# Layer 1's class tokens become the stationary operand, the atoms' weights move in a new stream layout, and the degrees are summed behind the norm's statistics

## The reference

```python
patch_out = gelu(patch_tokens @ fc1_w.T + fc1_b) @ fc2_w.T + fc2_b
gate_logits = einsum('bnd,nrd->bnr', l2norm(cls_tokens), l2norm(gate_pair)) + balance_bias
route_probs = softmax(gate_logits);  chosen_route = argmax(route_probs)
hid_all = gelu(einsum('bnd,ahd->bnah', cls_tokens, atom_in_w) + atom_in_b)
route_candidates = einsum('bnrh,nrdh->bnrd', sh_pair, route_out_w) + atom_out_b[dst]
cls_out = chosen_cand * chosen_w
```

## Time and profile before

| | us |
|---|---|
| median of 3 runs | 3323.42 (3315.17 to 3325.01) |
| profiled execution | 3323.25 |
| its span, first to last instruction | 3321.4 |
| TensorE busy | 3084.2 |
| DVE busy | 1713.4 |
| GpSimd busy | 1428.0 |
| ScalarE busy | 757.8 |
| mean granted TensorE clock | 0.952 of full |

### The profile page before, as it was taken

The page is one execution under the profiler, slowest core; times in us unless marked ns, Lnnn a source line. Parts: engine busy times, 40 slices in busy tenths (PEclk is TensorE's granted clock), DMA queues, the critical chain, the costliest instruction groups (busy, mean ns, idle before and its releaser), DMA issues.

```text
span 3321.4 us, 39056 instructions
## 1 busy us (share of the span) xinstructions
PE 3084.2 (93%) x14137; PEld 2434.6 (73%) x14147; DVE 1713.4 (52%) x2812; ACT 757.8 (23%) x1342; POOL 1428.0 (43%) x1007
## 2 busy tenths in 40 slices
PE   8999899999999977998997889899999998989978
PEld 3567577888888865776786578578888886778858
DVE  7734699565555355547765436533334436641141
ACT  1043211233323221103153122111111112221222
POOL 2022287435443451563430034356666664536600
PEclk9999999999999988999988789999999999999987
DMA  2011266212221121221210231122332232213303
GB/s 81 15 48 43 91 200 218 67 48 77 72 62 58 62 81 59 75 93 54 66 48 10 71 110 60 56 86 90 99 96 94 94 95 67 67 48 100 99 31 132
DMA packets 92134, 259.38 MB, mean 78 GB/s; under 512 B 10431, under 2 KB 11071, under 8 KB 91716
## 3 DMA queue, kind: packets, MB, share of 16 engines
q1 hardware_dynamic: 80352, 219.45, 20.9%
q10 hardware_dynamic: 11652, 38.19, 3.3%
HBM read 256.03 MB, written 1.57 MB: 78 GB/s over the span
## 4 chain that ended last, share of the span: by engine, by line
PE 85%; DVE 9%; issue 3%; ACT 2%; DMA 0%; ACTq 0%; DVEq 0%
PE ps L429 22%; PE ps L433 21%; PE ps L434 21%; PE ps L911 2%; DVE aux L1982 2%; PE ps L537 1%; PE ps L531 1%; PE ps L1245 1%; PE ps L997 1%; PE ps L1141 1%; PE ps L801 1%; PE ps L783 1%; PE ps L790 1%; PE ps L775 1%; DVE hot L2423 1%
## 5 line engine op out<-in xcount | busy, mean ns | idle before, releaser
L367 POOL TENSOR_SCALAR w_hi<-raw 128x768 fp32r<-128x768 f32 x498 | 462.4, 929 | 1680.4 <-PE ps L429 1451.8
L370 POOL TENSOR_TENSOR w_lo<-raw,w_hi 128x768 fp32r<-128x768 f32 x498 | 974.3, 1956 | 41.5
L429 PE MATMUL ps<-H_hi,w_hi 128*128 128x512 f32 x804 | 318.9, 397 | 21.1 <-issue 11.6
L429 PE MATMUL ps<-A_hi,w_hi 128*128 128x512 f32 x780 | 309.0, 396 | 12.1 <-ACT scr L1570 12.1
L434 PE MATMUL ps<-H_hi,w_lo 128*128 128x512 f32 x804 | 315.9, 393 | 0.0
L433 PE MATMUL ps<-H_lo,w_hi 128*128 128x512 f32 x804 | 315.8, 393 | 0.0
L429 PE MATMUL ps<-B_hi,w_hi 128*128 128x512 f32 x720 | 291.7, 405 | 21.0 <-DVE B_lo L1776 14.9
L433 PE MATMUL ps<-A_lo,w_hi 128*128 128x512 f32 x780 | 305.7, 392 | 0.0
L434 PE MATMUL ps<-A_hi,w_lo 128*128 128x512 f32 x780 | 305.1, 391 | 0.0
L433 PE MATMUL ps<-B_lo,w_hi 128*128 128x512 f32 x720 | 282.9, 393 | 0.0
L434 PE MATMUL ps<-B_hi,w_lo 128*128 128x512 f32 x720 | 282.8, 393 | 0.0
(11 more groups left out here) (480 smaller groups left out, 5857.5 us busy)
## 6 DMA issues: line engine op xcount, KB each, us to landing
raw<-stream_dram SPq DMA_DIRECT2D x558, 384.0 KB, 3.0
w_ring<-w_dram ACTq DMA_DIRECT2D x45, 384.0 KB, 3.6
u_rows<-rows_dram ACTq DMA_DIRECT2D x8, 768.0 KB, 5.8
rows<-rows_dram ACTq DMA_DIRECT2D x7, 768.0 KB, 3.8
w_last<-w_dram ACTq DMA_DIRECT2D x9, 384.0 KB, 3.6
x<-x_dram ACTq DMA_DIRECT2D x1, 1536.0 KB, 9.0
out_dram<-x ACTq DMA_DIRECT2D x1, 1536.0 KB, 5.1
orf<-orf_dram ACTq DMA_DIRECT2D x6, 192.0 KB, 3.1
```

Of the source, the lines that this page charges most:

```text
L367: pool.tensor_scalar(w_hi[:, b // 3, b % 3], raw[:, b // 3, b % 3], 1.0, 1.0, ALU.mult, ALU.mult)\
L370: pool.tensor_tensor(w_lo[:, b // 3, b % 3], raw[:, b // 3, b % 3], w_hi[:, b // 3, b % 3], ALU.subtract)\
L429: mm = pe.matmul(o, wh, xh, start=first, stop=False, skip_group_check=True)
```

## The change

- **Up.** A block now holds, for one chunk of 128 features and one half h, 128 columns of fc1 and 480 columns of the atoms' first weights. The chunk's 8 token columns become the stationary operand, and the 480 weight columns move: the class tokens come out as rows, in [8, 480] of banks 2 and 3, summed over the six chunks. fc1 keeps its form (128x128 weights, 512 columns), but goes chunk by chunk, so it begins with the first normed chunk. The gates' matmuls stand behind the fourth block.
- **Between.** DVE copies the class rows out of PSUM, ten transposes bring them to [96, 80] in bank 5, DVE adds the biases there and ScalarE takes one GELU where it took ten. Four DVE operations apply the route weights where twelve did.
- **Down.** fc2 comes first, from two blocks. Then come ten blocks with 96 rows of use, 768 columns each: the 8 hidden columns are stationary, and the weights move in two halves of 384 columns into banks 0 and 1, as rows. The biases go the same way in two matmuls. DVE copies the rows out, six transposes turn them, and one addition goes to `x`.
- **Degrees.** DVE prepares the counts before `gat_sum`. TensorE sums them (bank 4) behind the norm's second sum and `unpend()`. The copy, the root and the reciprocal stand within DVE's and ScalarE's work on the gates, and the scaling of the counts stands in front of the route weights.

```diff
 
             def degrees():
-                pe.wait_ge(dve_to_pe, S.due(dve_to_pe))
-                use(0)
-                for m in range(NT):
-                    mm = pe.matmul(ps[:, 0], ones[:, :], counts_f[:, m], start=m == 0, stop=m == NT - 1, skip_group_check=True)
-                done(mm, 0, "dve")
+                for m in range(NT):
+                    mm = pe.matmul(ps[:, 4], ones[:, :], counts_f[:, m], start=m == 0, stop=m == NT - 1, skip_group_check=True)
+                done(mm, 4, "dve")
 
             def to_nodes(src):
 
...
+                pe.wait_ge(dve_to_pe, counts_made)
+                degrees()
...
+                def raw_at(b):
+                    return raw[:, b // 3, b % 3].rearrange("p k c -> p (k c)")
+
+                def class_gates():
+                    pe.wait_ge(dve_to_pe, S.due(dve_to_pe))
+                    for k in range(KC):
+                        mm = pe.matmul(ps[:, 6, 0:30], ones[:, :], aux[:, k % 4, (k // 4) * 32:(k // 4) * 32 + 30],
+                                       start=k == 0, stop=k == KC - 1, skip_group_check=True)
+                    done(mm, 6, "dve")
+
+                turn = first_turn("ffn1")
+                for i in range(2 * KC):
+                    k, h = i // 2, i % 2
+                    w = raw_at(i % 6)
+                    whole_block(turn + i // 6, i % 6)
+                    if h == 0:
+                        pe.wait_ge(dve_to_pe, normed[k])
+                    mm = pe.matmul(ps[0:8, 2 + h, 0:480], acc[:, k, 0:8], w[:, P:P + 480], start=k == 0, stop=k == KC - 1,
+                                   skip_group_check=True)
+                    if k == KC - 1:
+                        done(mm, 2 + h, "dve")
+                    else:
+                        raw_given_back(mm)
+                    mm = pe.matmul(ps[:, h], w[:, 0:P], acc[:, k], start=k == 0, stop=k == KC - 1, skip_group_check=True)
+                    if k == KC - 1:
+                        done(mm, h, "act")
+                    whole_block_used()
+                    if i == 3:
+                        class_gates()
+                for q in range(2 * ATOMS):
+                    if q % ATOMS == 0:
+                        use(2 + q // ATOMS)
+                    mm = pe.transpose(ps[0:FF // 2, 5, q * 8:q * 8 + 8], scr[0:8, 4 + q // ATOMS, q % ATOMS * 96:q % ATOMS * 96 + 96],
+                                      ident[0:8, 0:8])
+                    raw_given_back(mm)
+                done(mm, 5, "dve")
+                for k in range(2):
+                    whole_block(turn + 2, k)
+                for f in range(KC):
+                    use(f)
+                    for k in range(2):
+                        if f == 0:
+                            pe.wait_ge(act_to_pe, S.due(act_to_pe))
+                        mm = pe.matmul(ps[:, f], raw_at(k)[:, f * P:f * P + P], scr[:, k], start=k == 0, stop=k == 1,
+                                       skip_group_check=True)
+                        raw_given_back(mm)
+                    done(mm, f, "dve")
+                whole_block_used()
+                whole_block_used()
                 pe.wait_ge(dve_to_pe, S.due(dve_to_pe))
-                for k in range(KC):
-                    mm = pe.matmul(ps[:, 6, 0:30], ones[:, :], aux[:, k % 4, (k // 4) * 32:(k // 4) * 32 + 30],
-                                   start=k == 0, stop=k == KC - 1, skip_group_check=True)
-                done(mm, 6, "dve")
-                turn = first_turn("ffn1")
-                for n in range(2):
-                    for f in range(KC):
-                        q = 6 * n + f
-                        c = slice(0, N if q < 2 else 8)
-                        whole_block(turn + n, f)
-                        use(f)
-                        for k in range(KC):
-                            if q == 0:
-                                pe.wait_ge(dve_to_pe, normed[k])
-                            mm = pe.matmul(ps[:, f, c], raw[:, f // 3, f % 3, k], acc[:, k, c], start=k == 0,
-                                           stop=k == KC - 1, skip_group_check=True)
-                            if k == 0:
-                                raw_given_back(mm)
-                        done(mm, f, "act")
-                        whole_block_used()
-                degrees()
-                pe.wait_ge(dve_to_pe, S.due(dve_to_pe))
-                for n in range(2):
-                    for f in range(KC):
-                        whole_block(turn + 2 + n, f)
-                        if n == 0:
-                            use(f)
-                            for k in range(2):
-                                if f == 0:
-                                    pe.wait_ge(act_to_pe, S.due(act_to_pe))
-                                mm = pe.matmul(ps[:, f], raw[:, f // 3, f % 3, k], scr[:, k], start=k == 0, stop=k == 1,
-                                               skip_group_check=True)
-                                if k == 0:
-                                    raw_given_back(mm)
...
+                    use(h)
+                    mm = pe.matmul(ps[0:8, h, 0:384], cls_w[:, :], atom_b[:, h * 384:h * 384 + 384], start=True, stop=False,
+                                   skip_group_check=True)
+                    raw_given_back(mm)
+                for q in range(2 * ATOMS):
+                    b = q + 2
+                    whole_block(turn + 2 + b // 6, b % 6)
+                    for h in range(2):
+                        mm = pe.matmul(ps[0:8, h, 0:384], scr[0:96, 3, q * 8:q * 8 + 8], raw_at(b % 6)[0:96, h * 384:h * 384 + 384],
+                                       start=False, stop=q == 2 * ATOMS - 1, skip_group_check=True)
+                        if q == 2 * ATOMS - 1:
+                            done(mm, h, "dve")
+                        else:
+                            raw_given_back(mm)
+                    whole_block_used(q == 2 * ATOMS - 1)
+                use(6)
                 for f in range(KC):
-                    mm = pe.matmul(ps[:, 6, 96 + f * 8:104 + f * 8], atom_b[:, f * P:f * P + P], cls_w[:, :], start=True,
-                                   stop=True, skip_group_check=True)
+                    if f % 3 == 0:
+                        use(f // 3)
+                    mm = pe.transpose(ps[:, 6, f * 8:f * 8 + 8], scr[0:8, 4 + f // 3, f % 3 * P:f % 3 * P + P], ident[0:8, 0:8])
                 done(mm, 6, "dve")
...
                 act.dma_start(atom_b[:, :], t["atom_b"]).then_inc(sel_in, 16)
                 act.dma_start(route[:, :], t["route"]).then_inc(sel_in, 16)
                 act.wait_ge(dve_to_act, S.due(dve_to_act))
+                act.activation(row[:, :], row[:, :], ACT.Sqrt).then_inc(act_to_dve, 1)
+                act.wait_ge(dve_to_act, S.due(dve_to_act))
                 act.activation(rt[:, 1, 12:30], rt[:, 0, 12:30], ACT.Sqrt).then_inc(act_to_dve, 1)
                 act.wait_ge(dve_to_act, S.due(dve_to_act))
                 act.activation(rt[:, 3, 0:6], rt[:, 2, 0:6], ACT.Exp).then_inc(act_to_dve, 1)
-                for q in range(12):
+                act.activation(junk[:, 7:8], ones[0:1, 0:1], ACT.Gelu)
+                for q in range(2):
                     act.wait_ge(tile_for["act"], S.due(tile_for["act"]))
-                    b = col("L1_ffn_in_b", q)
-                    if q < 2:
-                        freed(act.activation(scr[:, q], ps[:, q], ACT.Gelu, bias=b), q)
-                        mark(act_to_pe)
-                    else:
-                        freed(act.activation(scr[:, 2, q * 8 - 16:q * 8 - 8], ps[:, q % 6, 0:8], ACT.Gelu, bias=b), q % 6)
-                mark(act_to_dve)
+                    freed(act.activation(scr[:, q], ps[:, q], ACT.Gelu, bias=col("L1_ffn_in_b", q)), q)
+                    mark(act_to_pe)
                 act.wait_ge(dve_to_act, S.due(dve_to_act))
-                act.activation(row[:, :], row[:, :], ACT.Sqrt).then_inc(act_to_dve, 1)
+                act.activation(scr[0:96, 2, 0:80], scr[0:96, 2, 0:80], ACT.Gelu).then_inc(act_to_dve, 1)
...
-            def degrees():
+            def loop_counts():
...
-            def scaled_counts():
+            def degrees():
 
                 dve.wait_ge(tile_for["dve"], S.due(tile_for["dve"]))
-                freed(dve.tensor_copy(row[:, :], ps[:, 0]), 0)
+                freed(dve.tensor_copy(row[:, :], ps[:, 4]), 4)
                 mark(dve_to_act)
+
+            def degree_roots():
...
+            def degree_columns():
+
...
+            def scaled_counts():
...
@@ -2562,6 +2593,8 @@
                 target_rows()
                 edge_weights()
                 inverse_sums()
+                if "ffn1" in parts:
+                    loop_counts()
                 gat_sum("L1_gnn_b2")
             if "ffn1" in parts:
                 norm(x, acc, None, 1e-5)
@@ -2574,9 +2607,11 @@
                     dve.tensor_tensor(o[:, 12:24], g3[:, k], g3[:, k], ALU.mult)
...
```

(89 more changed lines are left out.)

## The result

The changed kernel takes 3296.43 us, the median of 8 runs (3289.25 to 3302.91), where the kernel before, run beside it, takes 3319.30 (8 runs, 3306.15 to 3325.84). The ratio is 0.9938 [0.9920, 0.9955]: faster, by 22.9 us between the medians. Its profiled execution took 3296.41 us, 26.8 less than that of before.

The account below looks back on a forecast made before the run. The prediction took TensorE's queue to bound layer 1's feed-forward stage, with small-column work lowering its clock. Its terms summed to 33.6 us saved, from 3323.25 to 3289.7 us (chance 0.72), range 3283 to 3301.

Parts of the forecast that it names:

- (c): fc1 in the up blocks: 12.8 us, partly at the low clock, become 10.3; gain 2.5 us.
- (d): Class matmuls of the up blocks: 20.3 us become 9.7 at the full clock; gain 10.6 us.
- (b): Gates' matmuls behind the fourth up block: 1.3 us at the full clock instead of 2.74, without a wait.
- (f): Ten new transposes of 8 rows between up and down: a loss of 1.1 us, bounds 0.9 and 2.
- (h): Biases and classes down, 22 narrow matmuls: 20.3 us become 14.3; gain 6.0 us.
- (j): The next norm's sums behind the stage: 7.35 us become 5.2 at the full clock; gain 2.2 us.
- (a): Start of the up blocks: first matmuls wait only for the first acc chunk, 1850.7 instead of 1858.1; gain 7.4 us.
- (e): Degrees moved behind the norm's statistics, into TensorE's idle time: 7.4 us gained; without that cover they would cost 3.4.
- Rival 1: The clock falls in the classes down only: 14.3 us become 23.1, total 3298.5 us; chance 0.08.
- Rival 3: Clock low from the first up block through the next norm's sums: slower than before, 3341.7 us; chance 0.03.
- Rival 2: DMA supply of weight blocks falls short: 2 to 4 us, total 3292 to 3294; chance 0.12 together with Rival 4.
- Rival 4: Gates' chain or GELUs late, TensorE waits at the transposes: 2 to 4 us, 3292 to 3294; 0.12 with Rival 2.

Follow-up runs that it names:

- gates_first: The changed kernel with the gates' six matmuls in front of the up blocks again: 3302.38 us in one run, stage 82.61 us against 75.17.
- degrees_back: The changed kernel with the degrees' matmuls and scaling back between up and down: 3308.16 us in one run, stage 80.29 us against 75.17.
- up_snake: The changed kernel with the up blocks' matmuls reordered, 6 changes of width instead of 23: 3294.75 us, ratio to before 0.9927, stage 72.79 us.
- up_wide128: The changed kernel with 128 stationary token columns instead of 8 in the up blocks' class matmuls: 3293.86 us, ratio to before 0.9905, stage 71.90 us.

## Why the prediction was right, and where it was off

The direction, the mechanism and the place of the gain were as forecast: TensorE's queue set the stage's length, and the lower clock level went from it. That the total came within 7 us is in part luck: the long stretch at the end was long in both profiled executions, so it cancelled. From the first block to the end of the next norm's sums the forecast had 53.6 us, and the trace has 57.1:

| | forecast | measured |
|---|---|---|
| first block behind the first acc chunk | 0 | 0.14 |
| twelve up blocks, (c) and (d) | 12 x 1.67 = 20.0 | 12 x 1.96 = 23.5 |
| gates (b) | 1.3 | 1.26 |
| transposes (f) | 1.1 | 0.57 |
| fc2 (g) | 10.3 | 10.50 |
| biases and classes down (h) | 14.3 | 14.39 |
| tail (i) | 1.4 | 1.39 |
| L531 (j) | 5.2 | 5.43 |

**The term that was mis-sized** is the block in (c) and (d). I took its price from rows in which all weights have one width, and the change makes the width alternate with each matmul. None of the rows that I read showed such an alternation of long matmuls, and the prediction didn't bound it. It costs 3.5 us, nearly the whole 3.7 in the stage.

**(a) and (b), start and gates:** 6.0 us of wait and gates by gates_first, where 6.1 were forecast. The 1.5 us more that this run costs are the first pair at the lower level, which the forecast counted in (c).

**(e), degrees:** they ran from 1847.99 to 1851.66, covered as said. They gave more than their 3.4 us of matmul: 5.1 by degrees_back, because without them the first pair ran at the lower level. The prediction took the full clock from the first block on as given and didn't name what keeps it.

**Rival 1**, a low clock in the last stretch, did not occur: 1.00 over 14.40 us in which 8-wide weights alone are at work. **Rival 3** fell with it: nothing in the stage ran at half clock. The router's rows had pointed the right way. **Rival 2:** no wait of TensorE's in the stage ends on a DMA, at 250 GB/s over the last stretch. The Trainium skill's 358 GB/s per core in "DMA: Bandwidth & Descriptors", Specifications, is not reached over a whole stretch (286 at most); over the 1.5 us from 1891.5 the trace shows 401, above it. **Rival 4:** DVE waited for TensorE and not the other way, by its timeline:

```profile
1874.67 0.65 DVE L2640 COPY scr<-ps 8x480 f32<-8x480 f32 x1 [4.44 <-PE ps L1145]
1876.63 0.65 DVE L2640 COPY scr<-ps 8x480 f32<-8x480 f32 x1 [1.31 <-PE ps L1145]
```

The first copy had 4.44 us to spare where 2 were forecast. The surplus comes from the blocks' slower pace: ten of them, each 0.29 us longer, stand ahead of this tile.

**The idle columns** of the Trainium skill, "TensorE: Matmul & The Clock Gate", Part 3, cost nothing by themselves: 480 columns on 8-wide weights take 0.83 us in up_snake, a change of width in every four included, and on 128-wide ones 0.80 in up_wide128.

**The total** was 6.7 us above the forecast. Besides the 3.7 in the stage, 3.0 lie outside it. The prediction read its own span as typical and took everything outside the stage as fixed, where an untouched stretch varies by some 15 us between executions. The 3.0 themselves are not of that stretch, which was long in both traces; 2.0 of them lie ahead of the stage, where two traces of one kernel differ by 2.2 us (before) and 6.6 (after). Their cause stays open. That the median shown and the profiled execution agreed within 0.2 us said only that both were in the upper group.

## What to carry to other kernels

In this kernel, 8 useful columns moved over full-width weights cost twice: the weight loads set the pace, and the granted clock stood at its lower level in that work and in the work behind it. The remedies that worked were to make the small operand the stationary one, or simply to move more columns: useless columns shortened a stage or steadied the total in three edits here (a fourth, 64 stationary columns, made the stage 0.5 us longer). Keep the stationary width the same from one matmul to the next. Look for waits of several microseconds ahead of long TensorE work, and fill them with small work that has to be done anyway. And measure a stage between two marks in the trace when another stretch makes the totals jump.

## What the runs showed of the hardware that I had not expected

- A change of the stationary width, 8 or 64 against 128, keeps the next weight load from starting early. With 8 it costs about 0.09 us at the narrow matmul and 0.20 at the wide one, 0.29 per pair. In one place a change of rows, 5 to 96 at 8 columns, did it too.
- In stretches of float32 records on 128x128 weights the granted clock averaged 0.64 and 0.62 with 8 moving columns, though TensorE was busy for 20.30 of 20.30 and 16.21 of 16.30 us. It was 1.00 with 128 in the same stretch, and with 64 it was 0.54 in one execution and 1.00 in another (38.7 or 22 us for 192 records).
- Over 14.40 us of 8-wide weights alone, with 384 moving columns, the granted clock was 1.00; so it was over the 24.80 us in which 8-wide weights with 480 columns alternate with full-width ones.
- Behind an idle time of 5.6 to 5.8 us TensorE came back at 0.51 to 0.52; behind the 1.1 us left in the changed kernel, between the degrees and the blocks, it stayed at 1.00.
